# Causal attention: the mask added to the scores by key is replaced by zeros that GpSimd writes over the probabilities

## The reference

```
q, k, v = split(layernorm(x) @ W_attn.T + b_attn)     # x: 4 batches x 512 x 256, 16 heads of 16
q, k = q * f, k * f                                   # f: a factor by position and feature
att = einsum('bhqd,bhkd->bhqk', q, k) / 4
att = where(causal, att, finfo.min)                   # no key after its query
y = einsum('bhqk,bhkd->bhqd', softmax(att), v)
x = x + y @ W_proj.T + b_proj
```

## Time and profile before

| | |
|---|---|
| median of 3 runs | 1884.54 us (1882.66 to 1884.92) |
| the profiled execution | 1883.69 us, of which its span 1881.9 us |
| engine busy over the span | PE 85%, DVE 65%, ACT 49%, POOL 33% |
| the causal block | from about 10 us to about 305 us of the span |

### The profile page before, as it was taken

One profiled execution on the slowest core, in us unless ns is written; L12 is line 12 of the kernel. 1 busy time (PEld: TensorE's weight loads), 2 busy tenths in 40 slices (PEclk: granted clock), 3 DMA queues, 4 the chain that ended last, 5 costly groups with the idle time before them and its releaser, 6 DMA issues. The chain is left out here.

```text
span 1881.9 us, 32646 instructions
## 1 busy us (share of the span) xinstructions
PE 1593.4 (85%) x11328; PEld 1155.5 (61%) x11328; DVE 1218.0 (65%) x2035; ACT 930.5 (49%) x1746; POOL 625.7 (33%) x863
## 2 busy tenths in 40 slices
PE   4889986858899997588888977887747999999996
PEld 2445443558899997233333332222247999999995
DVE  3566552444578886477777468777764777777773
ACT  1345452122156664145545657667711666666662
POOL 5444420010036654633344334333011233333321
PEclk8899998968899999689999988887855999999998
DMA  5222211121158885522212312222033677677763
GB/s 139 49 44 57 47 36 34 56 67 37 49 170 234 231 236 132 132 65 41 52 40 57 64 33 62 48 48 51 1 114 117 192 210 219 198 208 217 199 185 84
DMA packets 192834, 200.21 MB, mean 106 GB/s; under 512 B 33121, under 2 KB 167778, under 8 KB 192642
## 3 DMA queue, kind: packets, MB, share of 16 engines
q1 hardware_dynamic: 156578, 155.12, 28.0%
q0 software_dynamic: 36096, 43.04, 12.2%
HBM read 139.52 MB, written 22.54 MB: 86 GB/s over the span
## 5 line engine op out<-in xcount | busy, mean ns | idle before, releaser
L648 ACT ACTIVATE l1a_sb_probs<-l1a_s_ps,l1a_sb_kmax 128x512 f32<-128x512 f32 x256 | 173.0, 701 | 83.5 <-issue 52.2
L1668 PE MATMUL l1m_g_ps<-l1m_sb_rows_hi,l1m_sb_hi 128*128 128x256 f32 x736 | 209.2, 284 | 1.4 <-DVE l1m_sb_rows_lo L1550 1.4
L1668 PE MATMUL l1m_g_ps<-l1m_sb_rows_hi,l1m_sb_lo 128*128 128x256 f32 x736 | 208.9, 284 | 0.0
L1668 PE MATMUL l1m_g_ps<-l1m_sb_rows_lo,l1m_sb_hi 128*128 128x256 f32 x736 | 208.9, 284 | 0.0
L452 POOL DMA_DIRECT2D l1a_sb_kst<-l1a_sb_hi x256 | 125.7, 496 | 248.2 <-PE l1a_s_ps L768 197.6
L549 DVE TENSOR_REDUCE l1a_sb_mx<-l1a_s_ps 128x2 f32<-128x1024 f32 x128 | 154.0, 1219 | 62.2 <-PE l1a_s_ps L731 62.0
L583 DVE TENSOR_REDUCE l1a_sb_kmax<-l1a_s_ps 128x2 f32<-128x1024 f32 x128 | 153.0, 1217 | 41.1 <-PE l1a_s_ps L768 40.8
L654 ACT ACTIVATE l1a_sb_probs<-l1a_s_ps 128x1024 f32<-128x1024 f32 x128 | 128.0, 1023 | 88.3 <-PE l1a_s_ps L768 87.9
L768 PEld LDWEIGHTS l1a_s_ps<-l1a_sb_qst,l1a_sb_kst 49*128 49x128 f32 (+1 forms) x512 | 50.4, 197 | 176.2 <-issue 94.2
L549 DVE TENSOR_REDUCE l0a_sb_mx<-l0a_s_ps 128x2 f32<-128x256 f32 (+3 forms) x128 | 103.4, 821 | 80.1 <-PE l0a_s_ps L742 78.7
L768 PE MATMUL l1a_s_ps<-l1a_sb_qst,l1a_sb_kst 49*128 49x512 f32 (+1 forms) x512 | 131.0, 518 | 28.4 <-ACT l1a_sb_probs L648 23.7
(11 more groups left out here) (339 smaller groups left out, 4198.6 us busy)
## 6 DMA issues: line engine op xcount, KB each, us to landing
l1m_sb_raw<-in_l1m_w SPq DMA_DIRECT2D x184, 256.0 KB, 3.6
l0m_sb_raw<-in_l0m_w SPq DMA_DIRECT2D x96, 256.0 KB, 3.6
l1m_sb_raw<-in_l1m_w SPq DMA_DIRECT2D x23, 1024.0 KB, 6.4
l0m_sb_raw<-in_l0m_w SPq DMA_DIRECT2D x24, 512.0 KB, 4.7
l1a_sb_qst<-l1a_sb_hi SPq DMA_DIRECT2D x256, 32.0 KB, 2.1
l1a_sb_kst<-l1a_sb_hi POOLq DMA_DIRECT2D x256, 32.0 KB, 2.0
l0a_sb_qst<-l0a_sb_hi SPq DMA_DIRECT2D x128, 32.0 KB, 2.1
l0a_sb_kst<-l0a_sb_hi POOLq DMA_DIRECT2D x128, 32.0 KB, 2.1
```

What stands on the lines that cost most here:

```text
L648: ins = act.activation(probs[:, n % 8, e, :], at[:, e, :], ACT.Exp, bias=kmax[:, n % 4, e:e + 1], accum_out=zsum[:, n % 4, e:e + 1])
L1668: ins = pe.matmul(at, s, m, start=n == 0, stop=n == len(passes) - 1)
```

## The change

The four mask matmuls of each step `S` go away, and the tile `mask_k` with them (one third of the constant `halves` that is loaded at the start, and one cast on DVE). A new step `CUT` is put into the schedule for GpSimd, at every second j ahead of `S`: it waits for the second exponential of a key tile (`exp_done`), then one `affine_select` on 128 partitions x 4 heads x 128 queries keeps a probability where query >= key and writes 0 elsewhere. `PV` waits for `probs_cut` where it waited for `exp_done`. The mask in step `A` stays.

```diff
@@ attention_slot
     for j in range(2 * NT):
+        if kinds[b] == "causal" and j % 2 == 0 and (j or has_last):
+            yield "CUT", *((b, g) if j else last), (j - 2) // 2 % NT
         yield "S", b, g, j
@@ attention_schedule, behind the last slot
     yield "W", b, g, NT - 1
+    yield "CUT", b, g, NT - 1
@@ gpsimd
+            zero = pool.to_reg(0.0) if causal else None
+            def cut(b, g, kt):
+                if not causal:
+                    return
+                n = 8 * g + 2 * kt
+                exp_done.wait(pool, b, n + 1)
+                at = probs[:, n % 8:n % 8 + 2, :, kt * P:(kt + 1) * P]
+                pool.affine_select(at, at, [[0, 2], [0, 2], [1, P]], ALU.is_ge, zero, base=0, channel_multiplier=-1
+                                   ).then_inc(probs_cut.sem, 1)
-            run({"LN1": ln, "LN2": bias, "STACK": stack, "V": v_group})
+            run({"LN1": ln, "LN2": bias, "STACK": stack, "V": v_group, "CUT": cut})
@@ tensor, scores_by_key
-                                    start=True, stop=not causal)
-                if causal:
-                    ins = masked(at[:, :, c0:c0 + P], "mask_k")
+                                    start=True, stop=True)
@@ tensor, probs_v
-                exp_done.wait(pe, b, 8 * g + 2 * kt + 1)
+                if causal:
+                    probs_cut.wait(pe, b, NT * g + kt)
+                else:
+                    exp_done.wait(pe, b, 8 * g + 2 * kt + 1)
@@ load_constants, vector
-            for n, half in enumerate((ident_b, mask_q, mask_k)):
+            for n, half in enumerate((ident_b, mask_q)):
```

More of the change, by code:

```diff
@@ L300, in attention @@
         exp_done = steps("exp_done", 8 * NG)
+        probs_cut = steps("probs_cut", NT * NG if causal else 0)
         pv_done = steps("pv_done", NT * NG)
@@ L836, in load_constants @@
     minus_half, eps = sb("minus_half", [P, NT]), sb("eps", [P, NT])
-    halves = sb("halves", [P, 3, 2, P])
+    halves = sb("halves", [P, 2, 2, P])
     iota = sb("iota", [P, 32])
@@ L844, in load_constants @@
         const[f"sum{n}"] = nc.dram_tensor(f"sum{n}_dram", (B * T + BLK, D), F32, kind="Internal").ap()
-    ident_b, mask_q, mask_k = (sb(n, [P, 2, P], BF16) for n in ("ident_b", "mask_q", "mask_k"))
+    ident_b, mask_q = (sb(n, [P, 2, P], BF16) for n in ("ident_b", "mask_q"))
     before_b, ones_b = (sb(n, [P, P], BF16) for n in ("before_b", "ones_b"))
@@ L876, in _ @@
             dve.memset(ones_b[:, :], 1.0).then_inc(made, 1)
-            dve.wait_ge(made, 8)
+            dve.wait_ge(made, 7)
     return const
@@ L1876, in layout @@
     a["rope"] = np.tile(rope_factor().T, (P // HD, 1))
-    whole = np.stack([a["ident"], np.where(at[None] > at[:, None], NEG, 0),
-                      np.where(at[None] < at[:, None], NEG, 0)]).astype(np.float32)
-    a["halves"] = np.tile(whole.reshape(3, 2, P // 2, P).transpose(2, 0, 1, 3), (2, 1, 1, 1))
+    whole = np.stack([a["ident"], np.where(at[None] > at[:, None], NEG, 0)]).astype(np.float32)
+    a["halves"] = np.tile(whole.reshape(2, 2, P // 2, P).transpose(2, 0, 1, 3), (2, 1, 1, 1))
     a["iota"] = np.tile(np.arange(32, dtype=np.float32), (P, 1))
```

## The result

The changed kernel takes 1893.45 us (median of 5 runs, 1891.9 to 1896.18); the kernel before took 1884.92 beside it (5 runs). The ratio is 1.0045, 95% interval 1.0033 to 1.0058: slower by 0.45%, 8.5 us. The profiled execution took 1892.68 us with a span of 1891.0, so it stands 9.1 us of span above the one of before. Two executions among the experiments ran in a far slower state (3901 us in "aside", 2558 us in the changed kernel again); the medians and ratios given leave them out.

The account below looks back on a forecast made before the run. PE's queue in the first block was taken to set the pace. Slot, end and start terms summed to +1.7 us, one clock dip added +1.5, together +3.2 on 1883.69: 1887 us, range 1878 to 1904.

Parts of the forecast that it names:

- What is removed: Masks by key on PE: about 0.1 us less each step S, 0.8 us a slot, 12.8 us for 16 slots.
- What is added: 64 selects on POOL at 1.28 us each, 82 us in total, fitting into POOL's idle 130 us.
- c: Time of one affine_select of 512 elements on POOL: taken as 1.28 us, low end 0.51, high end 2.36.
- rival 1: The select on POOL is cheap (0.51 us) and the change pays: -6.4 us, 1877.3 us; chance 0.23.
- dip: A fall of PE's granted clock to half; the one at 292 us was taken to cost some 1.5 us.
- Where it stands: PV 0 waits for CUT 0 behind STACK's DMAs: net +6.4 us for two slots g = 0, +1.4 at block's end.
- The clock: PE's granted clock falls to half once, with two new waits of 3.5 us on PE: +1.5 us.
- rival 3: PE's clock falls at most of the nine new waits and not at one: +12 us, 1899 us; chance 0.05.
- Rival 4: PE's queue is not shortened, masks ran in the shadow of the scores' weight loads: +8 us, 1895 us; chance 0.05.

Follow-up runs that it names:

- aside: The changed kernel with its 64 selects run over a tile of their own, TensorE waiting for exponentials alone: 1881.26 us, ratio 0.9969 to the kernel before.
- no cut: The changed kernel without its 64 selects, so no masks by key either, PV waiting for exponentials: 1882.42 us, ratio 0.998 to the kernel before.
- split: The changed kernel with STACK's 12 DMA issues on GpSimd in two halves placed around the selects: 1886.77 us, ratio 0.9999 to the kernel before.
- mix: Selects only on key tiles 1 to 3 of ten slots, masks kept elsewhere (all slots g = 0 included): 1879.74 us, ratio 0.9966 to the kernel before.

## Why the prediction was right, and where not

I said 1887.0 us, the range 1878 to 1904, and slower as the likeliest of the three signs; measured were 1893.45 us and slower. That is luck in good part: the select's price was taken twice too high and the clock's far too low, and these errors offset each other in part. So the points matter more than the sum.

- **What is removed.** The step from the first S to the first A shortened by 0.09 us as said, but a slot gains 0.3 to 0.75 us and not 0.8, and the first slot nothing: "no cut" gained 4.5 us where I had 13.3. In its profile the slots before the last two and the start gained 7.9, and the clock at the end took 4.3 back. The masks left PE's queue, and a part of it turned into waits for exponentials, 11.7 us against 8.3, which I had said would stay as long. Why slots g = 0 and 1 gain less than g = 2 and 3 was not tested.
- **What is added.** c was 0.64 us, not 1.28. The row of the memset (0.51), my low end, was the nearer one, and the adds, with two inputs, were the wrong neighbours. By my own terms this is rival 1's ground: about -6 us without a dip, 1877.7.
- **Where it stands.** Right: PV 0 waits for CUT 0 behind STACK. 2.8 us in b1g0 (3.5 - 0.64 would be 2.9); 0.44 in b2g0, most of it swallowed since PE was late by then. None in slots g = 2, as the chain of the earlier trace rows gives with 0.64. Slot g = 3 I had as just in time by 0.03 us; with 0.64 it had 0.9 us to spare, and the pause of 1.76 us in the issue of DMAs used that up and made PV 0 0.9 us late, within its wait of 1.61. At the end 0.24 us.
- **The clock.** This step failed by its size: I charged one dip at 1.5 us. Against the kernel before, the slots b0g0, b1g0, b1g3 and b2g0 of the profiled execution are longer by 3.6, 4.4, 2.7 and 2.9 us and the end by 2.8, +16.4 together; the eleven other slots are shorter by 6.8 and the start by 0.6. That makes the +9.0 of the profiles. Against "no cut", which has the gains alone, the four slots are longer by 14.9 us, of which 4.8 are waits for selects that the rows show (4.1 without the part of b1g3's wait in which the division was not done either); the rest is mostly work at half clock, some of it where there is no wait for a select (b0g0). The end's 2.8 us do not come from a select either: "no cut" has 3.3 there. The mechanism is near that of rival 3, to which I gave 0.05, but the clock fell at two of the waits for selects and not at most of nine, and the second stretch, through b1g3 and b2g0, lasted 17 us where I priced a dip at 1.5. The argument against it, that PE waits 0.5 to 1.3 us in each slot at full clock, held up to a point: the clock fell in the new waits of 1.6 and 2.8 us, and in other profiles ("split", "aside") also behind the wait of 1.59 us for the x add.
- **Rival 4** is wrong: PE's queue did get shorter. Its sum also leaves out the 0.3 us kept in each of the two slots g = 0; with them it is +8.8, not +8.

What is shown: the loss in the total is there only if TensorE waits for the selects ("aside", "no cut"), and most of it goes when the selects get out from behind STACK ("split"). What stays open: why the first slot is 3 us longer in the changed kernel and not in "aside", though no wait for a select stands in it; what decides how long a stretch at half clock lasts and whether a wait of 1.6 us starts one; and whether masks at the block's end help the clock there.

## What to carry to other kernels

A step moved to an idle engine is priced by the queue that it stands in, and not by its duration alone: look for the issues of DMAs ahead of it, and leave room for their pauses. Where TensorE sets the pace, a new wait of 1.5 to 3 us is to be priced with several microseconds of half clock behind it, and with a scatter as large; a move of work that only just fits should be made only for those tiles that no matmul waits for, as in "mix". And two kernels that differ by less than 10 us here can't be told apart by the total of one profile each: the same instructions took 17.9 and 23.5 us at the end of this block, and 608.6 and 618.9 us in the blocks `l1a` (from one block's first statistics to the next's).

## What the runs showed of the hardware

- An affine_select of 512 elements for each of 128 partitions takes 0.64 us on GpSimd, 1.25 ns an element, where the add with two inputs takes 2.3 (1024 elements) to 2.9 (256).
- A select slows an operation of DVE beside it. Kernel after, POOL and DVE in order of time:

```profile
138.43 0.64 POOL L481 TENSOR_SCALAR_AFFINE_SELECT l0a_sb_probs<-l0a_sb_probs 128x512 f32<-128x512 f32 x1 [5.13 <-ACT l0a_sb_probs L670]
138.50 1.11 DVE L555 TENSOR_TENSOR l0a_sb_lo<-l0a_sb_qk,l0a_sb_hi 128x512 fp32r<-128x512 f32 x1
```

  In "no cut" the same subtraction takes 0.69 us:

```profile
L555 DVE TENSOR_TENSOR l0a_sb_lo<-l0a_sb_qk,l0a_sb_hi 128x512 fp32r<-128x512 f32 x16 | 11.0, 688 | 5.0 <-ACT l0a_sb_hi L648 5.0
```

  The page SBUF — State Buffer of the Trainium skill (section SBUF: two separate sides) calls the port pair that DVE and GpSimd share an exclusive lock, also for a DVE operation with two inputs in SBUF against a GpSimd operation that reads SBUF. The row nearly agrees: the select ends at 139.07, and the subtraction ends 0.54 us later, most of its own 0.69.
- The granted clock stayed at half from 182.5 to 199.6 us behind a wait of 1.61 us, with PE busy 13.61 of 14 us in the middle of it.
- Behind the same wait of 1.59 us, the same matmuls ran at full clock in one execution (1.98 us) and at half in another (3.68).
